# Expert outputs added in DRAM: two sums per token in place of four rows

## What is computed

```python
scores = sigmoid(xt @ gate_w.T)                  # xt: 8192 tokens x 256
_, idx = top_k(scores + gate_b, 4)               # 4 of 16 experts for each token
w = take(scores, idx); w = w / w.sum() * 2.5
for e in range(16):                              # silu(gate) * up, 128 wide, then down to 256
    y = y + comb[:, e][:, None] * (silu_and_mul(xt @ w13[e].T) @ w2[e].T)
y = y + silu_and_mul(xt @ w13_s.T) @ w2_s.T      # one expert that all tokens share
out = x2 + gate * y                              # x2: what the mixer gave
```

## Time and profile before

| | us |
|---|---|
| median of 3 runs | 1802.29 (1800.54 to 1802.88) |
| span of the profiled execution | 1934.6 |

### The profile page before, as it was taken

How to read it: one execution, slowest core, us unless ns; L and a number is a source line. 1 busy time by engine, 2 the same in 40 slices (tenths; PEclk the granted TensorE clock), 3 DMA queues, 4 the chain that set the end, 5 groups by cost and what they waited for, 6 DMA issues and landing times. The chain is left out here.

```text
span 1934.6 us, 35851 instructions
## 1 busy us (share of the span) xinstructions
PE 1609.3 (83%) x10690; PEld 1343.0 (69%) x10690; DVE 1323.2 (68%) x3304; ACT 1107.9 (57%) x2311; POOL 982.6 (51%) x940
## 2 busy tenths in 40 slices
PE   6749999999999999999999886258888787786798
PEld 4337777777777777777777775147778777776565
DVE  6647788888888888888888776524444444443588
ACT  4535767676767676676767565435555545554222
POOL 2103345565565656565655556735555555555443
PEclk9869999999999999999999998579999999999899
DMA  8620111121121222121221113755555455552998
GB/s 280 213 73 22 38 35 57 60 73 66 65 74 59 69 70 70 61 79 58 71 69 62 66 49 109 233 153 157 153 160 168 148 166 158 157 155 87 355 400 321
DMA packets 149272, 237.88 MB, mean 123 GB/s; under 512 B 27788, under 2 KB 96140, under 8 KB 148912
## 3 DMA queue, kind: packets, MB, share of 16 engines
q1 hardware_dynamic: 123200, 165.83, 27.3%
q0 software_dynamic: 25344, 69.50, 9.7%
q10 hardware_dynamic: 544, 0.26, 0.0%
HBM read 128.28 MB, written 109.35 MB: 123 GB/s over the span
## 5 line engine op out<-in xcount | busy, mean ns | idle before, releaser
L2141 POOL DMA_INDIRECT ys_dram<-byo,bids x272 | 260.9, 959 | 256.4 <-DVE bids L2121 156.7
L1580 DVE SCALAR_TENSOR_TENSOR cv<-xc,convw,cv 128x256 f32<-128x256 f32 x576 | 300.1, 588 | 14.2 <-ACT cv L1421 13.9
L1055 POOL DMA_INDIRECT xs_dram<-rows,dest x256 | 267.5, 1045 | 77.6 <-issue 74.4
L115 PE MATMUL bank<-wh,bhh 128*128 x544 | 161.5, 297 | 78.1 <-ACT bhh L2046 67.5
L2094 DVE TENSOR_TENSOR bhl<-bank,bhh 128x512 fp32r<-128x512 f32 x136 | 94.1, 692 | 192.5 <-ACT bhh L2046 181.5
L2046 ACT ACTIVATE bhh<-bank 128x512 fp32r<-128x512 f32 x136 | 83.5, 614 | 182.2 <-PE bank L1979 173.0
L115 PEld LDWEIGHTS bank<-wh,bhh 128*128 128x128 f32 x544 | 103.5, 190 | 91.4 <-issue 91.3
L116 PE MATMUL bank<-wl,bhh 128*128 x544 | 154.4, 284 | 1.4 <-issue 1.4
L117 PE MATMUL bank<-wh,bhl 128*128 x544 | 154.2, 284 | 0.8 <-issue 0.8
L115 PE MATMUL bank<-hTh,win_hi 128*128 128x256 f32 x384 | 115.4, 301 | 16.7 <-POOL hTl L1823 10.5
L1270 PE MATMUL bank<-xdt,dec 128*128 128x64 f32 x1024 | 122.6, 273 | 5.7 <-DVE dec L1606 5.7
(11 more groups left out here) (272 smaller groups left out, 5268.9 us busy)
## 6 DMA issues: line engine op xcount, KB each, us to landing
bx<-xs_dram SPq DMA_DIRECT2D x272, 129.0 KB
cy<-ys_dram SPq DMA_DIRECT2D x32, 1024.0 KB, 12.8
px<-in_x SPq DMA_DIRECT2D x16, 512.0 KB, 5.4
h_t<-phT SPq DMA_DIRECT2D x16, 512.0 KB, 3.6
hT<-h_t SPq DMA_DIRECT2D x32, 256.0 KB
xr<-in_x SPq DMA_DIRECT2D x32, 256.0 KB
x_dram<-xr SPq DMA_DIRECT2D x32, 256.0 KB, 2.0
h_dram<-h SPq DMA_DIRECT2D x32, 256.0 KB
```

The costliest lines, as they stand in the source:

```text
L115: pe.matmul(out, a_hi, b_hi, start=start, stop=False, skip_group_check=True)
L1055: pool.indirect_dma_start(out=xs_dram[:, :], out_offset=bass.IndirectOffsetOnAxis(ap=dest[p][:, CH * b + c, k:k + 1], axis=0), in_=rows[b] ...
L1580: dve.scalar_tensor_tensor(cv[b][:, m, :], xc[b][:, m, tap:tap + GROUP], convw[:, m, tap:tap + 1], cv[b][:, m, :], ALU.mult, ALU.add).then ...
L2141: pool.indirect_dma_start(out=ys_dram[:, :], out_offset=bass.IndirectOffsetOnAxis(ap=ids[u % XBUF][:, n:n + 1], axis=0), in_=yo[u % YBUF][ ...
```

## The change

`ys_dram` holds two rows per token, `SUMS = 2`, in place of four. The first block of a pair adds its rows to sum 0 of its tokens and the second adds to sum 1; the scatter is an accumulating DMA (`compute_op=ALU.add`). All four choices of a token carry the same target now, token x 2, and `take_ids` adds n to it. Within a block of one expert a token stands once at most. Two scatters in flight that add to the same row would lose a sum, so before scatter n of pair u GpSimd waits until scatter n of pair u - 1 has landed (`added[n]`). The waits of ACT and DVE on `y_out` become waits on both `added` semaphores with the same distance in pairs.

The sums must begin at zero: during the mixer SP issues 32 DMAs, one in each half that has a `second` part, that copy a tile of zeros over `ys_dram` (24576 rows of 1 KB in all, 768 in each), behind `store`. The last stage loads two rows of a token, DVE adds them, and one matmul adds the result to the bank.

```diff
+SUMS = 2
+YROWS = (NB * SEQ + 2 * NE * P) * SUMS
...
+                        pool.memset(nothing[:, :], 0.0)
...
+                def clear_sums(b, i):
+                    n = (i - 1) * NB + b
+                    sp.dma_start(ys_dram[n * CLEARED:(n + 1) * CLEARED, :].rearrange("(p r) d -> p r d", p=P),
+                                 nothing[:, :].unsqueeze(1).to_broadcast([P, CLEARED // P, D])
+                                 ).then_inc(sums_cleared, 16)
...
                     if tail and not located:
                         store(*tail)
+                    if second:
+                        clear_sums(*second)
...
+                sp.wait_ge(sums_cleared, 16 * NB * STEPS)
...
                     if u >= YBUF:
-                        act.wait_ge(y_out[u % YBUF], 32 * (u // YBUF))
+                        for n in range(SUMS):
+                            act.wait_ge(added[n], 16 * (u - YBUF + 1))
...
                     dve.tensor_copy(ws[u % XBUF][:, :], x[u % XBUF][:, :, D + 1])
-                    dve.tensor_copy(ids[u % XBUF][:, :], x[u % XBUF][:, :, D]).then_inc(ids_done, 1)
+                    for n in range(SUMS):
+                        last = dve.tensor_scalar(ids[u % XBUF][:, n:n + 1], x[u % XBUF][:, n, D:D + 1], float(n), None,
+                                                 ALU.add)
+                    last.then_inc(ids_done, 1)
...
-                    for n in range(2):
+                    for n in range(SUMS):
+                        if u >= 1:
+                            pool.wait_ge(added[n], 16 * u)
                         pool.indirect_dma_start(
                             out=ys_dram[:, :],
                             out_offset=bass.IndirectOffsetOnAxis(ap=ids[u % XBUF][:, n:n + 1], axis=0),
-                            in_=yo[u % YBUF][:, n, :], in_offset=None).then_inc(y_out[u % YBUF], 16)
+                            in_=yo[u % YBUF][:, n, :], in_offset=None, compute_op=ALU.add).then_inc(added[n], 16)
...
                     sp.dma_start(y[n % YBUF][:, :, :, :],
-                                 ys_dram[n * 2 * P * TOPK:(n + 1) * 2 * P * TOPK, :].rearrange(
-                                     "(c p k) d -> p c k d", c=2, k=TOPK)).then_inc(y_in[n % YBUF], 16)
+                                 ys_dram[n * 2 * P * SUMS:(n + 1) * 2 * P * SUMS, :].rearrange(
+                                     "(c p k) d -> p c k d", c=2, k=SUMS)).then_inc(y_in[n % YBUF], 16)
...
-                        for m in range(2):
-                            last = pe.matmul(TOTAL[n % 4][:, :].rearrange("p (c d) -> p c d", c=2), ident[:, :],
-                                             pair[n % 2][:, :, m, :], start=False, stop=(m == 1),
-                                             skip_group_check=True)
-                        last.then_inc(total_ps, 1)
+                        pe.matmul(TOTAL[n % 4][:, :].rearrange("p (c d) -> p c d", c=2), ident[:, :],
+                                  pair[n % 2][:, :, :], start=False, stop=True,
+                                  skip_group_check=True).then_inc(total_ps, 1)
...
-                    dve.tensor_tensor(pair[n % 2][:, :, :, :], y[n % YBUF][:, :, 0:2, :], y[n % YBUF][:, :, 2:4, :],
+                    dve.tensor_tensor(pair[n % 2][:, :, :], y[n % YBUF][:, :, 0, :], y[n % YBUF][:, :, 1, :],
                                       ALU.add).then_inc(pair_done, 1)
```

More of the change, by code:

```diff
@@ L104, in build @@
         mixer(nc, sem, taken, clear_semaphores, tables, t, mod, gate_b_row, gate_ln, ident, minus_half, bank, run, h_dram, h2_dram, par_dram,
-              cs_dram, x2_dram, xs_dram)
+              cs_dram, x2_dram, xs_dram, ys_dram)
         clear_semaphores()
@@ L126, in prepare_tokens @@
 def prepare_tokens(nc, sem, t, mod, gate_b_row, gate_ln, ident, minus_half, bank, win, wout, wglu, after, far, convw,
-                   convb, skip_w, glub, route_consts, counts, ends_i, state, xc, best, run, first_tiles, h_dram,
+                   convb, skip_w, glub, route_consts, counts, ends_i, state, xc, best, nothing, run, first_tiles, h_dram,
                    par_dram, cs_dram, xs_dram):
@@ L673, in mixer @@
 def mixer(nc, sem, taken, clear_semaphores, tables, t, mod, gate_b_row, gate_ln, ident, minus_half, bank, run, h_dram, h2_dram, par_dram,
-          cs_dram, x2_dram, xs_dram):
+          cs_dram, x2_dram, xs_dram, ys_dram):
     with ExitStack() as ctx:
@@ L708, in mixer @@
         ones = kept("ones", [P, P])
+        nothing = kept("nothing", [P, D])
         earlier = kept("earlier", [P, P])
@@ L773, in mixer @@
                        [(ones, "ones"), (earlier, "earlier"), (gatew, "gate_w"), (gateb, "gate_b"), (slot0, "slot0"),
-                        (tail_of, "tail_of")], early_counts, ends_i, state, xc, best, run,
+                        (tail_of, "tail_of")], early_counts, ends_i, state, xc, best, nothing, run,
                        ([tiles[1] for tiles in hT], hT_in, par[0], par_in[0], ends_j, [pair[0] for pair in ends_in]),
@@ L844, in mixer @@
         half_a = [x[:, 0, :].rearrange("p (k t) -> p k t", k=KD) for x in xend]
+        sums_cleared = sem("sums_cleared")
+        CLEARED = YROWS // (NB * STEPS)
         held_dve = sem("held_dve")
@@ L1035, in assign @@
             dve.tensor_scalar(dest[p][:, :, :], place[:, :, 0:TOPK], -1.0, None, ALU.add)
-            dve.tensor_scalar(tail_of[:, :, :, 0], tail_of[:, :, :, 0], float(GROUP * TOPK), None, ALU.add)
+            dve.tensor_scalar(tail_of[:, :, :, 0], tail_of[:, :, :, 0], float(GROUP * SUMS), None, ALU.add)
             dve.tensor_tensor(run[:, :], run[:, :], msum[:, :], ALU.add)
@@ L1938, in blocks @@
         x_in = [sem(f"b_x_in{n}") for n in range(XBUF)]
-        y_out = [sem(f"b_y_out{n}") for n in range(YBUF)]
+        added = [sem(f"b_added{n}") for n in range(SUMS)]
         (xT_ps, hh_done, hl_done, up_ps, gs_done, ff_done, fT_ps, fh_done, fl_done, down_ps, yo_done, ids_done) = (
@@ L2143, in _ @@
                             out_offset=bass.IndirectOffsetOnAxis(ap=ids[u % XBUF][:, n:n + 1], axis=0),
-                            in_=yo[u % YBUF][:, n, :], in_offset=None).then_inc(y_out[u % YBUF], 16)
-                for n in range(YBUF):
-                    pool.wait_ge(y_out[n], 32 * (PAIRS // YBUF))
+                            in_=yo[u % YBUF][:, n, :], in_offset=None, compute_op=ALU.add).then_inc(added[n], 16)
+                for n in range(SUMS):
+                    pool.wait_ge(added[n], 16 * PAIRS)
 def combine(nc, sem, gate_b_row, ident, bank, sh, sl, kept, h2_dram, x2_dram, ys_dram, out):
@@ L2167, in combine @@
         fl = several(2, "cfl", [P, MGROUP], F32R)
-        pair = several(2, "cpair", [P, 2, 2, D])
+        pair = several(2, "cpair", [P, 2, D])
         total = several(2, "ctotal", [P, 2, D])
@@ L2432 @@
     xs_dram = nc.dram_tensor("xs_dram", (ROWS, RW), F32, kind="Internal").ap()
-    ys_dram = nc.dram_tensor("ys_dram", (NB * SEQ * TOPK + 2 * NE * P, D), F32, kind="Internal").ap()
+    ys_dram = nc.dram_tensor("ys_dram", (YROWS, D), F32, kind="Internal").ap()
     build(nc, t, x2_dram, h_dram, h2_dram, par_dram, cs_dram, xs_dram, ys_dram, out)
```

8 lines of the change are left out of this document (4 added, 4 removed).

## The result

| | us |
|---|---|
| before, beside it | 1802.35 (1800.54 to 1802.88) |
| changed kernel | 2060.09 (2045.52 to 2068.96) |
| ratio | 1.1428 (1.1398 to 1.1457) |
| predicted | 1883.6, range 1772 to 2035 |

The direction was right, the size was not: the loss is 258 us where 81 were forecast, and the time lies above the range. The profiled execution took 2068.96 us and its span is 2067.2.

A forecast was written before the change was run, and what follows sets the result against it. The prediction took TensorE to bound the block loop (2.80 us a pair) and the last stage. Its sum was 1802.3 + 108.8 (scatters waiting in the loop) - 27.5 (matmuls saved) = 1883.6 us, range 1772 to 2035.

The forecast's parts named there:

- p = 3.05: Block loop: p is the time per pair, from one scatter's start to its successor's; 3.05 us was the forecast's lower case.
- Mixer: Mixer: the 32 added clearing DMAs cost 0 us, bounds 0 to 16 us; DMA share from 0.20 to about 0.27.
- Block loop, form: Block loop: GpSimd waits for the previous pair's scatter to land, and this chain replaces TensorE's 2.80 us as the pace.
- The rival of a chain under 2.80 us: Block loop: a scatter follows its predecessor in under 2.80 us, so only the gain is left, 1774.8 us; chance 0.17.
- Block loop, size: Block loop: 3.60 us a pair against 2.80, over 136 pairs, costs +108.8 us; at 4.7 us a pair +258.
- last byte to the next start: Block loop: 0.7 us from a scatter's last byte to the semaphore, then 0.30 to the next start.
- traffic: Block loop: two loads of 129 KB and the other chain's scatter share the DMA engines, taken as 0.25 us.
- adding is serial: Block loop: DMA engines read, add and write each row before the next, 6.0 us a pair, 2210 us; over 4.7: chance 0.15.
- Last stage: Last stage: one matmul in place of two saves 27.5 us on TensorE, a group falling from 7.60 to 5.88 us.
- The gaps: Block loop: the profile's 3.64 us a pair holds gaps of the profiled execution, 114 us; undisturbed runs go at 2.80.
- the gaps are real in the timed runs too: Block loop: timed runs also stand at 3.64 us a pair, hiding the chain of 3.60; result 1775 us; chance 0.05.
- The forecast span of 1907 us: Whole profiled execution: its loop is already at 3.64 us a pair, so the span becomes 1934.6 - 27.5, about 1907 us.

The follow-up runs named there:

- e5_after: The changed kernel run again on the second chip, beside the kernel before: 2061.8 us, ratio 1.1453.
- e6_before: The kernel before, unchanged, a single run on the second chip: 1801.7 us.
- e1_plain_chain: The changed kernel with plain scatters in place of adding ones, all waits kept, sums left out; first chip: 1923.3 us, ratio 1.0023.
- e9_add_free: The kernel before with adding scatters to four rows per token and clears in the mixer, no scatter waiting for another; third chip: 1928.0 us, ratio 1.0699.
- e11_after_dve: The whole changed kernel with GpSimd's two splits of the last stage done by DVE; third chip: 2052.4 us, ratio 1.1368 to the kernel before.
- e0_before: The kernel before, unchanged, a single run on the first chip: 1919.1 us.
- e4: The kernel before with only the last stage changed, two of four expert outputs left out, GpSimd's two splits there on DVE: 1775.7 us, ratio 0.9854.
- e10: The kernel before with only the last stage changed, two of four expert outputs left out; third chip: 1796.6 us, ratio 0.9973.

## Why the prediction was wrong in size, point by point

**The sum, redone.** On the second chip, e5_after against e6_before by spans: start of the scatters -3.0 us (1269.0 for 1272.0), loop +258.1, tail -5.3, together +249.8 = 2049.7 - 1799.9. The prediction had 0, +108.8 and -27.5. Of the 176 us missing, some 150 to 170 are the loop and 22 the last stage. The forecast's own range has a slip besides: its lower end, 1836, is p = 3.05 without the gain; by the prediction's own terms it is 1802.3 + 34 - 27.5 = 1809.

**Mixer: right.** Clears cost nothing. TensorE is busy 795.17 of 850 us, against 795.5 in e6_before, and the first scatter comes no later. The share was forecast at 0.27 and is 0.28.

**Block loop, form: right.** GpSimd's idle time is ended by landings of the scatters and ACT waits for ys_dram, two scatters to a pair, the loop at the pace of a chain through DRAM. The rival of a chain under 2.80 us is dead: e1_plain_chain shows that even a plain link takes 3.17 us where little else moves.

**Block loop, size: this is the step that failed.** The sum for the time from a scatter's start to its successor's start was mis-sized: 3.60 us, where 4.70 to 4.83 were measured. Term by term, an adding link:

| term | predicted, us | measured, us |
|---|---|---|
| issue on GpSimd | 0.96 | 1.56 |
| to the first byte | 0.52 | about 0.5 |
| moving, adding included | 0.37 + 0.5 | 1.12 |
| last byte to the next start | 0.7 + 0.30 | about 1.35, what is left of 4.53 |
| traffic | 0.25 | 0.17 to 0.30, what is left of 4.70 to 4.83 |
| sum | 3.60 | 4.70 to 4.83 |

The measured start-to-last-byte is 1926.14 - 1922.98 = 3.16 us, taking the last window as 0.28 x 0.5 full; 4.53 less that is about 1.35. The last two rows of the table are remainders, not readings, and the second joins two executions. The largest miss, 0.60 us, is the issue. It was left at 0.96 in the sum although the text of a rival said that it might grow. The same miss sits in a second candidate for the pace, GpSimd's own issues: it stood there as 2 x 1.26 = 2.52 us, below TensorE's 2.80, and is 3.72 (e9_add_free), above it. The other two are adding at 1.12 us in place of 0.87, and the way from last byte to start, 0.35 over the estimate; the plain link shows the latter too (3.17 = 0.96 + about 0.5 + 0.37 + about 1.3). In the loop the plain link takes 0.48 us more than in thin traffic (3.65 for 3.17); what makes that is open. Each is a piece that no row of before showed, and each came out on the same side. The upper end, 4.7, was built as if the issue were known, and so the range ended where the measurement begins.

The Trainium skill, page "DMA: Bandwidth & Descriptors", "Anatomy of one DMA — SWDGE (gpsimd) path", has a fixed 2.0 us and the bytes at 436 GB/s, from which the prediction worked out 3.56 us as an estimate for a plain scatter. The trace has 3.17 in quiet and 3.65 in the loop, on either side of it. For the adding one, 4.53 to 4.64 in quiet, that estimate is too low by 1 us.

**The rival "adding is serial".** It stood at 6.0 us with 0.15. Right in direction, too far in size: the packets are three times as many (144 for 48) and the moving is three times as long (1.12 for 0.37), not 2.4 us more. Its other sentence, that growing issue alone might take the loop over, is what e9_add_free shows, with 1.56 in place of the 2.0 us supposed.

**Last stage: wrong, on a step that was named.** "Nothing overtakes TensorE, though DVE comes close." DVE's 5.0 us a group were worked out from mean durations, and these means carried stretched instructions; they shrink only for the work removed, while GpSimd's two subtractions go on stretching one addition each. The condition "if the group stays above 6.5 us (the gain isn't on TensorE)" is met, at 7.75. TensorE's part itself was right: 5.90 us for 5.88 once DVE is freed (e11_after_dve, where DVE also does GpSimd's two splits), and 25 us of the 27.5 appear. What was missing is a look at the spread. The kernel before shows it already, in the lines of its pair sums and its last addition (min/median/max in ns):

```profile
L2294 DVE TENSOR_TENSOR cpair<-cy x32: 1211/1218/3361, 1805.7 to 1926.2; 128x1024 f32<-128x1024 f32 x32
```
```profile
L2318 DVE TENSOR_TENSOR x_kept<-x_kept,ctotal x26: 691/693/1711, 1815.0 to 1910.1; 128x512 f32<-128x512 f32 x26
```

The medians look undisturbed and the longest instances are 2.8 and 2.5 times as long.

**The gaps: right pace, wrong reason.** 2.80 us a pair is what timed runs have beside 1802 us (e6_before 2.79, span 1799.9). But the prediction gave the gaps to the profiled execution. A profiled execution without gaps (e6_before) and 19 timed runs at 1915 to 1925 us beside one with them (e0_before, 3.57 us a pair) show that profiling isn't what makes them; they go with the chip or the batch, which one batch a chip can't tell apart. Which chip the first profile came from is not recorded, and its 1934.6 us lie above all of these runs, so that this one execution stays unexplained. The 114 us that the prediction read for its gaps were right: its loop is (1784.8 - 1291.5) - 378.1 = 115 us longer than that of e6_before. Another 20 us lie ahead of the first scatter (1291.5 for 1272.0), where the prediction thought that hardly anything could hide. The rival "the gaps are real in the timed runs too" is wrong for the runs at 1802 us and right on the first chip, though its 1775 us was tested by no run. The forecast span of 1907 us, with its "gain in the profile, loss in the times", failed: the changed kernel's span is 2067.2, beside a time of 2068.96. The difference between unchanged runs on the first and second chip is 117 us by spans, of which the loop has (3.57 - 2.79) x 135.5 = 106 and the time before the first scatter 11 (1283.4 for 1272.0). What makes the gaps is open.

**Open.** The changed kernel's pace differs from execution to execution, 4.70 and 4.83 us a pair in two profiles (e5_after and the first; 4.88 in e11_after_dve, whose loop is the same), and 2045 to 2073 us in its eight times. No run here shows why. A version that beats the kernel before with all four outputs was not found: e4 and e10 gain with work left out.

## What to carry to other kernels

A scatter that adds cost more here than one that writes, in its issue (1.56 for 0.96 us) and in moving (1.12 for 0.37): before one enters a dense loop, measure its issue on GpSimd and the time from one to its dependent successor in a loop of their own, since both can bound the pace. A wait that takes the place of independent writes costs its whole excess over the loop's pace, in every iteration, and a once-only gain elsewhere (27.5 us of matmuls) is small beside 136 times one microsecond. And before work is taken off the bounding engine, look in the timeline at the longest instances on the next one, not at its mean.

## What the runs showed of the hardware that was not expected

- An indirect scatter of 128 rows of 1 KB holds GpSimd 0.96 us plain and 1.56 us with adding (medians of 272), takes the 16 DMA engines 0.37 us and 1.12 us, and has 48 and 144 packets (worked out from the queue's totals).
- A scatter that waits for its predecessor follows it after 3.17 us plain and 4.53 to 4.64 us adding, in thin traffic; in the loop after 3.65 and 4.70 to 4.88.
- A DVE addition of 128x512 with both inputs in SBUF takes 0.69 us, and 2.88 when it starts 0.03 us behind a GpSimd subtraction of 2.37 us. When it starts 0.10 us ahead of one, it keeps its 0.69, and the subtraction takes 1.75 us in place of 1.29. DVE did the larger subtraction in 1.22 us, GpSimd in 2.37.
- Three chips ran the same kernel at 1801.8, 1802.1 and 1918.9 us. Of the 117 us between the spans of the second and the first 106 lie in one loop, whose TensorE is busy 369.69 of 375 us on the second.
